# A second level of Strassen's scheme under two of seven gate/up products, with seven narrow sub-products spread among the plain slots

## What is computed

```
x = x + attention(layernorm(x), ctx)          # x (8, 256, 1024), f32
n = layernorm(x)
Wg, Wu = dequant(gate_q), dequant(up_q)       # (3584, 1024), 16-value codes, a scale for each block of 64
Wd = dequant(down_q)                          # (1024, 3584)
g = einsum('bsh,mh->bsm', n, Wg)
u = einsum('bsh,mh->bsm', n, Wu)
out = x + einsum('bsm,hm->bsh', silu(g) * u, Wd)
```

## Times and the profile before

| | us |
|---|---|
| median of 3 runs | 1918.14 |
| lowest, highest | 1915.06, 1926.84 |
| the profiled execution | 1915.01 |
| its span in the trace | 1913.2 |
| gate and up stages without the first ten slots, in the span | 406.84 to 1401.83 |
| down projection | 1401.83 to the end |

### The profile page before, as it was taken

The page is one execution under the profiler, slowest core; times in us unless marked ns, Lnnn a source line. Parts: engine busy times, 40 slices in busy tenths (PEclk is TensorE's granted clock), DMA queues, the critical chain, the costliest instruction groups (busy, mean ns, idle before and its releaser), DMA issues.

```text
span 1913.2 us, 27653 instructions
## 1 busy us (share of the span) xinstructions
PE 1895.8 (99%) x9758; PEld 964.5 (50%) x9758; DVE 1221.6 (64%) x1980; ACT 1196.0 (63%) x2167; POOL 548.0 (29%) x802
## 2 busy tenths in 40 slices
PE   9999999999999999999999999999999999999999
PEld 4488888644444444444444444444444444444444
DVE  7966888848577577476476476485464234466963
ACT  3886776578876676777777777766696888200000
POOL 2013342303233243242242342241354333111110
PEclk9999999999999999999999999999999999999999
DMA  9247999956664465465564564554798999764462
GB/s 356 71 90 191 258 260 282 286 165 157 142 150 123 119 146 130 114 151 119 124 155 115 122 156 112 129 149 96 179 210 211 218 233 242 212 236 134 153 234 85
DMA packets 437754, 326.03 MB, mean 170 GB/s; under 512 B 371680, under 2 KB 371952, under 8 KB 435696
## 3 DMA queue, kind: packets, MB, share of 16 engines
q1 hardware_dynamic: 393568, 171.07, 41.0%
q0 software_dynamic: 43872, 153.12, 25.3%
q10 hardware_dynamic: 176, 0.07, 0.0%
HBM read 154.31 MB, written 82.31 MB: 124 GB/s over the span
## 4 chain that ended last, share of the span: by engine, by line
PE 89%; ACT 3%; issue 2%; DVE 1%; DMA 1%; POOL 0%; DVEq 0%; ACTq 0%; POOLq 0%
PE ps L2297 48%; PE ps L2340 26%; PE ps L1658 9%; PE ps L1693 2%; ACT sq L335 2%; PE ps L1626 2%; PE ps L1058 1%; DMA T<-keep_x 1%; PE ps L1597 0%; ACT tail L2382 0%; ACT tail L2371 0%; ACT sq L331 0%; DMA wS<-halves 0%; DVE tail L2504 0%; DMA scales<-in_L_ffn_down_q 0%
## 5 line engine op out<-in xcount | busy, mean ns | idle before, releaser
L2297 PE MATMUL ps<-T,wS 128*128 128x512 f16 x4704 | 1017.2, 379 | 10.9 <-ACT ps L2355 3.0
L2297 PEld LDWEIGHTS ps<-T,wS 128*128 128x128 f16 x4704 | 459.8, 98 | 565.2 <-issue 10.3
L335 ACT ACTIVATE sq<-sq 128x512 f32<-128x512 f32 x1176 | 658.5, 619 | 0.2
L2340 PE MATMUL ps<-T,tail 128*128 128x512 f16 x1584 | 344.7, 379 | 0.0
L2340 PEld LDWEIGHTS ps<-T,tail 128*128 128x128 f16 x1584 | 155.0, 98 | 186.9
L416 DVE SCALAR_TENSOR_TENSOR halves<-w,halves 128x512 f16<-128x512 f32 x240 | 173.0, 726 | 116.8 <-POOL halves L407 116.7
L407 POOL CAST halves<-w 128x512 f16<-128x512 f32 x215 | 172.5, 819 | 178.3 <-DMA wS<-halves 104.1
L2382 ACT CAST tail<-tail 128x512 f16<-128x512 f32 x187 | 115.0, 616 | 98.3 <-DVE tail L2413 62.6
L2231 POOL DMA_DIRECT2D keep_h<-tail x196 | 106.6, 545 | 224.8 <-DVE tail L2447 222.1
L2447 DVE SCALAR_TENSOR_TENSOR tail<-tail 128x512 f16<-128x512 f32 x196 | 146.1, 745 | 36.0 <-ACT tail L2382 30.2
L2340 PE MATMUL ps<-T,wS 128*128 128x512 f16 x768 | 168.4, 379 | 0.0
(11 more groups left out here) (238 smaller groups left out, 1652.6 us busy)
## 6 DMA issues: line engine op xcount, KB each, us to landing
keep_h<-tail POOLq DMA_DIRECT2D x196, 256.0 KB, 2.9
tail<-keep_h POOLq DMA_DIRECT2D x66, 512.0 KB, 5.1
wS<-keep_h POOLq DMA_DIRECT2D x32, 512.0 KB, 4.9
T<-in_x SPq DMA_DIRECT2D x13, 1024.0 KB, 8.1
q<-in_L_ffn_up_q POOLq DMA_DIRECT2D x50, 256.0 KB, 3.6
q<-in_L_ffn_gate_q POOLq DMA_DIRECT2D x48, 256.0 KB, 3.2
q<-in_L_ffn_down_q POOLq DMA_DIRECT2D x42, 256.0 KB, 4.3
keep_x<-T SPq DMA_DIRECT2D x38, 256.0 KB, 4.0
```

Of the source, the lines that this page charges most:

```text
L335: nc.scalar.activation(place, place, ACT.Prelu, bias=bias, scale=scale, alpha=alpha).then_inc(un.s_act, 1)
L2297: last = nc.tensor.matmul(ps[:, bank, :], un.wS[:, z % SLOTS, a, kt, :], t.Tp[side][product][:, :, b, kt, :], start=fresh and n == 0, stop ...
L2340: last = nc.tensor.matmul(ps[:, j, :], h[:, j // PAIRS, a, tok], quad(q, c)[:, b].rearrange("p k d -> p (k d)"), start=fresh and n == 0, s ...
```

## The change

From the third pair on (`JOINT_FROM = 2`, twelve of fourteen pairs), the products P1 and P5 of the gate and of the up stage are no longer made as such. P1 of both stages stacked is again a 2 x 2 block product on one activation form, and is made by seven sub-products (part A); P5 in the same way (part B). A sub-slot is 2 blocks of the inner dimension by 3 parts, 6 matmuls. A pair then has 34 slots: 20 of 12 matmuls and 14 of 6.

- PE: the order is in `joint_slots`; the sub-slots of a pair stand among the last slots of the pair before and the gate's slots.
- ACT: 14 copies a pair (`sub_copied`, `copied`), where there were 8.
- DVE: four additions more a pair (`sub_combined`), 16 weight sums instead of 8, eight of them 256 elements a lane (`joint_add`), and 17 low parts instead of 14. POOL casts and SP transposes 17 pieces instead of 14.
- Activation forms of the second level: eight are made once, during stages 1 to 3, at slots `FORM2_AT`: on DVE 20 operations of 1024 elements a lane (`form2_sum`) and 8 low parts (`form2_lo`), on ACT 8 casts. Six are stored in DRAM (`keep_f`) and loaded again in each pair, 512 KB each, by POOL into two buffers (`form2_load`).
- Rings: `SQ_RING` 4 to 3, `HALF_RING` 5 to 4. The gated forms' high part, low part and store are one and two units of 6 matmuls apart where they were one and two slots of 12.

```
-SQ_RING = 4
-Q_RING, HALF_RING, SLOTS = 3, 5, 9
+SQ_RING = 3
+Q_RING, HALF_RING, SLOTS, W_BUFS = 3, 4, 9, 10
...
+JOINT_FROM = 2
+PLAIN_STAGES = 2 * JOINT_FROM
+JOINT_PIECES = 17
...
+FORM2_AT = (15, 20, 25, 30, 35, 40, 46, 50)
+FORM2_OPS = (3, 2, 2, 3, 2, 2, 3, 3)
...
+def joint_slots(pair):
+
+    g, u, before = 2 * pair, 2 * pair + 1, 2 * pair - 1
+    return [(before, P3, 0), (g, P1, A), (before, P3, 1), (g, P5, A), (before, P4, 0), (g, P6, A), (g, P2, A), (before, P4, 1),
+            (g, P7, A), (g, P3, A), (g, P1, B), (g, P6, 0), (g, P5, B), (g, P6, 1), (g, P6, B), (g, P2, B), (g, P2, 0),
+            (g, P7, B), (g, P3, B), (g, P4, A), (g, P2, 1), (g, P4, B), (g, P7, 0), (g, P7, 1), (g, P3, 0), (g, P3, 1), (g, P4, 0), (g, P4, 1),
+            (u, P2, 0), (u, P6, 0), (u, P2, 1), (u, P6, 1), (u, P7, 0), (u, P7, 1)]
...
+    def sub_slot(pe, k, pair, product, part, z):
...
+        elif product in (P6, P2):
+            copy_done(pe, pair, A_V if part == A else B_V)
+        elif product in (P7, P3):
+            mid_done(pe, pair, A_U4 if part == A else B_U4)
+        else:
+            mid_done(pe, pair, A_U7 if part == A else B_U7)
...
+        if (product, part) in FORM2_USES:
+            n = len(FORM2_USES) * (pair - JOINT_FROM) + FORM2_USES.index((product, part))
+            pe.wait_ge(s_hl[n % 2], ring_count(n, 2))
...
+        todo = [(kt, a, b) for kt in range(2) for a, b in PARTS]
...
+    def sub_combined(dve, k, pair, product, part):
+
+        if (product, part) == (P6, A):
+            dve.wait_ge(s_mm, k + 1)
+            copy_done(dve, pair, A_P5)
+            nc.vector.tensor_tensor(ps[:, X + 1, :], ps[:, V, :], t.p1u[:, 0, :], ALU.add).then_inc(s_mid, 1)
...
+        def form2_load(n):
+            if n == 0:
+                pool.wait_ge(s_kept2, 16 * FORMS2_STORED)
+            if n >= 2:
+                pool.wait_ge(s_mm, FORM2_USE_AT[n - 2] + 1)
+            nc.gpsimd.dma_start(t.form2_rows[n % 2], t.x2[FORM2_OF_USE[n % len(FORM2_USES)]]).then_inc(s_hl[n % 2], 16)
```

More of the change, by code:

```diff
@@ new lines, with piece_of @@
+FIRST_JOINT = SLOT_AT[2 * JOINT_FROM - 1, P3, 0]
+JOINT_SLOTS = len(joint_slots(JOINT_FROM))
+WIDTH = [1 if part >= A else 2 for _, _, part in ORDER]
+START = [sum(WIDTH[:k]) for k in range(SLOT_COUNT + 1)]
+def piece_of(k):
+    stage, product, part = ORDER[k]
+    if stage < PLAIN_STAGES:
+        return PIECES * stage + product
+    first = PLAIN_PIECES + JOINT_PIECES * (stage // 2 - JOINT_FROM)
+    if part >= A:
+        return first + SUB_PIECE[part - A][product][0]
+    return first + MAIN_PIECE[stage % 2][product]
@@ L480, in __init__ @@
         d = 0
-        for stage in range(STAGES):
+        for stage in range(PLAIN_STAGES):
             u, z = 4 * stage, PIECES * stage
```

549 lines of the change are left out of this document (450 added, 99 removed).

## The result

| | before | after |
|---|---|---|
| median (9 runs each) | 1923.06 us | 1931.19 us |
| lowest, highest | 1915.06, 1926.84 | 1924.91, 1933.94 |
| profiled execution, its span | 1915.01, 1913.2 | 1924.91, 1923.1 |
| span: until slot 10 of the first stage | 406.84 | 411.98 |
| span: the stages from there to the first down matmul | 994.99 | 999.74 |

The ratio of after to before is 1.0047, with a 95% interval of 1.0028 to 1.0065. The forecast was 1892 us with a range of 1883 to 1914; both medians here lie above it. (The median of 1918.14 that the prediction starts from is that of the first three runs.)

A forecast was written before the change was run, and what follows sets the result against it. The prediction took the number of matmuls on PE, 0.2158 us each, as the bound. Its terms summed as 1915.0 - 30.9 - 3.0 + 5.5 + 4.4 = 1891.0 us, stated as 1892 in terms of the median, range 1883 to 1914.

The forecast's parts named there:

- What bounds the kernel: Gate and up stages: the number of matmuls on PE is the bound, each one removed giving 0.2158 us.
- part 1: Matmuls of the twelve joint pairs: 143 fewer at 0.2158 us each, -30.9 us.
- Part 2: Stall before P6 of stage 3, waiting for ACT's copy: goes as shorter rings leave out 18 activations, -3.0 us.
- Part 3: Making the eight second-level forms: DVE's long operations make PE wait in stage 2 and at first P7 A, +5.5 us.
- Part 4: Joint pairs in steady state: DVE's sum late at P7 A, 0.4 us in each of 11 further pairs, +4.4 us.
- rival (c): Second-level forms or pieces come late by DMA, 1 to 2 us late; 1903 to 1915 us, chance 0.13.
- Rival (b): DVE late in every joint pair, slowed beside POOL casts, 1.5 to 2 us a pair; 1909 to 1915 us, chance 0.17.
- Part 5: Hand-over and down steps: transposing down weights four steps ahead instead of six costs nothing, 2.30 us gap stays; 0.
- rival (d): POOL stuck behind a cast stores gated forms late; ACT, DVE, PE wait; twice a pair gives 1942 us; chance 0.10.
- The starting point: Profiled execution of the kernel before, 1915.0 us, taken as 3.1 us below the median of 1918.14.

The follow-up runs named there:

- the three traces of before: The kernel before, unedited, profiled three times: 1915.01, 1933.12 and 1922.65 us.
- the first trace: The changed kernel, unedited, profiled the first time: 1924.91 us, stages 999.7 us.
- the second: The changed kernel, unedited, profiled a second time: 1930.50 us, stages 1004.4 us.

## Why the prediction was wrong, step by step

- **What bounds the kernel, and part 1**: right. 143 matmuls went, the pitch stayed 0.2158 us, -30.9 us. Nothing in any trace goes at 131 ns a matmul.
- **Part 2**, -3.0 us: right. The gap ahead of P6 of stage 3 (2.97, 3.04 and 2.77 us in the three traces of before) is in no trace of the changed kernel.
- **Part 3**, +5.5 us: right in place and in the length of the operations, too large. The making costs 2.7 us ahead of the first joint pair, where I had 4, and 0.5 at its P7 A, where I had 1.5: pauses of DVE took up more of the 7.5 us than I allowed. Before, DVE waited 1.10, 0.80 and 0.91 us for ACT between 466 and 480 us; in after it works there without a pause. The new operations took 7.8 us: less 2.8 to spare and 2.8 of pauses that is 2.2, and PE waited 1.34 us for the first side's sum and 0.70 for the second's.
- **Part 4**, +4.4 us at P7 A: the step that failed. P7 A has no gap in the steady pairs. The shortest time was not that of DVE's sum but that of the load for P4, which I had put into rival (c) with a chance of 0.13. Its working had the right terms: 10.4 us from release to use, issue and 5.0 us of landing (measured 5.6 for P4 A and 6.3 for P4 B at the median). What failed above all is the delay ahead of the issue, 2.7 us from the mean wait of before. The changed program has more there: a cast that waits for a transpose until 0.8 us after the release, then takes 3.9 us beside DVE's work, and three issues of 0.54 us: 6.2 us. And it is the same in each pair, not now and then, so 1.1 to 2.1 us at P4 A came in each and up to 0.7 at P4 B in some; the inner pairs lost 28.3 us in the first trace, 2.57 a pair, 20.5 of it ahead of P4 A and P4 B. The wait that I did price, of DVE for ACT's high part (1.1 us), is there in ten of the eleven pairs with 0.93 us, but ahead of the sum for P7 B, where it costs PE 0.2 us a pair.
- **Rival (b)** priced a POOL cast as what slows DVE. It did: ahead of the sum for P7 B a low part and a sum of gated results take 0.97 and 1.09 us in ten inner pairs instead of 0.68, which is why PE waits those 0.2 us there. The larger effect went the other way, a cast held while DVE works.
- **Part 5**, 0: wrong by 8 us in the first trace and 12 in the second. I left the 2.30 us gap near 1352 as it was. The chain that made it was the very mechanism of rival (d), and I asked whether it would come with each pair, not what it would cost at its own place once stores and sums stand closer and a form load stands in the same queue. It came once, in the last pair, and cost 10.4 us.
- **The starting point**: I took one execution at 1915.0 as 3 us below the median. It was as fast as the fastest of the three runs, and the medians of before in the comparisons are 1921 to 1923. This is 3 to 5 us of the miss and no error of the sum.

By its own terms in the first trace: -30.9 - 3.0 + 2.7 + 28.3 + 8.1 = 5.2 us against the 4.75 measured in the stages, where I had -24.0. The rest of the difference between the two profiled executions, 5.1 us ahead of slot 10, lies within the 19 us by which that stretch varies in the kernel before.

The range took in (c) and the forecast, but not (c) together with (d) in the last pair; both happened, and both come from what stands ahead of an issue in POOL's program.
